# Closing the last chunk of a time-mixing layer in two halves, with the first expert's weights held behind its rows

## The reference

```python
# time mixing, per head
S = w_t * S + k_t v_t ;  y_t = r_t (S + u k_t v_t)
y = (y - mu) * rsqrt(var + eps) * ln_g + ln_b
x = layernorm(x + y @ W_o)                      # x1 below
# experts: capacity C = ceil(T * 2 / 32 * 1.2), T = 8192 tokens: 615 rows
top_w, top_i = top_k(softmax(x @ gate_w + gate_b), 2)
pos = how many earlier (token, choice) pairs took the same expert      # dropped if pos >= C
ye = gelu(xe @ w1 + b1) @ w2 + b2
x = layernorm(x + sum over the 2 choices of weight * ye)
```

## Time and profile before

| | |
|---|---|
| median of 3 runs | 2318.22 us (2316.73 to 2318.42) |
| the profiled execution | 2315.27 us, span 2313.5 us from first to last instruction |
| mean granted TensorE clock | 0.931 of full speed |
| busy share of the span | TensorE 83%, VectorE 78%, GpSimd 60%, ScalarE 47% |

### The profile page before, as it was taken

The page is one execution under the profiler, slowest core; times in us unless marked ns, Lnnn a source line. Parts: engine busy times, 40 slices in busy tenths (PEclk is TensorE's granted clock), DMA queues, the critical chain, the costliest instruction groups (busy, mean ns, idle before and its releaser), DMA issues. The chain is left out here.

```text
span 2313.5 us, 30790 instructions
## 1 busy us (share of the span) xinstructions
PE 1918.6 (83%) x9894; PEld 1327.6 (57%) x9894; DVE 1806.9 (78%) x3029; ACT 1097.8 (47%) x2143; POOL 1378.8 (60%) x954
## 2 busy tenths in 40 slices
PE   5887888787877878788865399999999999999980
PEld 2333343343433433333322299999999999999980
DVE  2899999999999999999995266666666666666655
ACT  2244554445444554445443255555555555555546
POOL 4667787777877887778874134444444444454440
PEclk9899999999999999999976599999999999999995
DMA  6832111121112111211110245554545545455537
GB/s 168 220 88 64 51 42 53 49 63 30 55 45 61 41 45 37 61 49 37 41 52 30 85 96 123 122 122 121 122 121 122 124 121 122 120 123 120 122 60 291
DMA packets 160569, 209.27 MB, mean 90 GB/s; under 512 B 12796, under 2 KB 136096, under 8 KB 160480
## 3 DMA queue, kind: packets, MB, share of 16 engines
q1 hardware_dynamic: 106544, 143.09, 21.1%
q0 software_dynamic: 28672, 34.78, 8.8%
q10 hardware_dynamic: 25264, 30.33, 4.9%
HBM read 118.65 MB, written 75.53 MB: 84 GB/s over the span
## 5 line engine op out<-in xcount | busy, mean ns | idle before, releaser
L801 DVE TENSOR_TENSOR_SCAN S<-wT,S,vb 128x512 f32<-128x512 f32 x512 | 624.9, 1262 | 0.0
L1075 POOL TENSOR_TENSOR prod<-S,rT 128x2048 f32<-128x2048 f32 x128 | 536.6, 4200 | 136.4 <-DVE S L801 135.8
L1294 PE MATMUL up<-x_parts,w_parts 128*128 128x308 f32 x3072 | 463.8, 307 | 1.5 <-DVE x_parts L1407 1.5
L1309 PE MATMUL down<-w_parts,h_parts 128*128 128x512 f32 (+1 forms) x1280 | 452.2, 396 | 0.0
L1294 PEld LDWEIGHTS up<-x_parts,w_parts 128*128 128x128 f32 x3072 | 438.9, 189 | 4.1 <-issue 1.8
L1369 POOL TENSOR_TENSOR ye<-ye,weight 128x256 f32<-128x256 f32 (+1 forms) x160 | 197.6, 1235 | 380.7 <-DVE ye L1463 380.7
L1347 ACT ACTIVATE h_full<-up,b_now 128x616 f32<-128x616 f32 x256 | 198.5, 776 | 420.8 <-PE up L1294 420.0
L1377 POOL DMA_INDIRECT sums<-ye,sum_at x160 | 283.8, 1773 | 146.5 <-POOL ye L1369 136.9
L1450 DVE TENSOR_TENSOR h_parts<-h_full,h_parts 128x616 fp32r<-128x616 f32 x256 | 206.7, 807 | 193.4 <-ACT h_parts L1347 193.2
L1312 PE MATMUL down<-w_parts,h_parts 128*128 128x256 f32 (+1 forms) x1280 | 357.3, 279 | 0.0
L794 DVE TENSOR_TENSOR vb<-vb,kT 128x512 f32<-128x512 f32 x512 | 327.9, 686 | 26.3 <-PE vb L575 26.2
(11 more groups left out here) (180 smaller groups left out, 2669.7 us busy)
## 6 DMA issues: line engine op xcount, KB each, us to landing
w_raw<-in_L_ffn_w_dram SPq DMA_DIRECT2D x64, 1024.0 KB, 8.8
expert_in_rows<-y_tok ACTq DMA_DIRECT2D x30, 652.5 KB, 9.2
xe<-expert_in_rows SPq DMA_DIRECT2D x32, 522.0 KB
v_stack<-v_parts SPq DMA_DIRECT2D x64, 256.0 KB, 4.5
x_tok<-in_L_attn_x_dram SPq DMA_DIRECT2D x16, 512.0 KB, 3.8
x_res<-in_L_attn_x_dram SPq DMA_DIRECT2D x16, 512.0 KB, 3.8
sums<-x_row SPq DMA_DIRECT2D x16, 512.0 KB, 2.9
rows<-sums SPq DMA_DIRECT2D x16, 512.0 KB, 6.8
```

Of the source, the lines that this page charges most:

```text
L801: dve.tensor_tensor_scan(line[:, 1:TC + 1], wT[:, par, half, :], vb[:, p % 2, g, :], line[:, 0:1], ALU.mult, ALU.add).then_inc(scanned, 1)
L1075: pool.tensor_tensor(prod[:, q % 2], S[:, q % RING, :, 0:TC], rT[:, par, half, None, :].to_broadcast([P, QUAD, TC]), ALU.mult).then_inc(pr ...
L1294: last = pe.matmul(up[:, f % 2, half, 0:HC], w1_parts[:, par, wp, k, f * P:(f + 1) * P], x_parts[:, par, xp, k, half * HC:(half + 1) * HC] ...
L1309: pe.matmul(down[0:m, (par * TILES + t) % 2, :, :], h_parts[:, 0, f, t * P:t * P + m], w2_parts[:, par, :, f, :], start=f == 0, stop=False)
```

## The change

The last chunk's closing steps no longer go through `stage_c`. Each engine has a `last_c` of its own, in which every step is done for two halves of two tiles, k = 0 and 1, each with a bank of `pa` (free by then; the gate uses banks of `vb`) and with 18 new semaphores. VectorE measures and normalizes both norms (statistics, inverse, one subtract-and-scale instruction for each tile), where ScalarE did most of that; ScalarE keeps roots, gain and bias, copies and weights. VectorE also works out the slot numbers. GpSimd is left with the copy of row numbers and the eight scatters, four behind each half. SP stores `x1` in two halves. The counters that only later chunks would need are left out. In `experts`, SP waits at expert 0 until both parts of its rows have landed before it issues `b2` and everything behind it.

```diff
@@ -409,11 +429,14 @@
-            store_x1(NCHUNK - 1)
-            sp.wait_ge(x1_stored, 16 * NCHUNK)
-
+            for k in range(2):
+                sp.wait_ge(half_normed, TPC + 2 * (k + 1))
+                sp.dma_start(sums[SPARE + (NCHUNK - 1) * TC + k * HALF:SPARE + (NCHUNK - 1) * TC + (k + 1) * HALF, :]
+                             .rearrange("(q p) c -> p q c", p=P), x1[:, 2 * k:2 * k + 2, :]).then_inc(x1_stored, 16)
+            sp.wait_ge(x1_stored, 16 * (NCHUNK + 1))
...
+        def chunks(eng, body, stage_a, tail):
...
             body(NCHUNK - 1, 1, False, True)
-            for s in range(SLOTS + 1):
-                stage_c(NCHUNK - 1, 1, s)
+            tail(NCHUNK - 1, 1)
...
@@ -611,11 +633,54 @@
 
-            def last_c(i, par, s):
-                if s == 0:
-                    for q in (NQ - 2, NQ - 1):
-                        reduce_y(i, par, q)
-                stage_c(i, par, s)
+            def last_c(i, par):
+                for q in (NQ - 2, NQ - 1):
+                    reduce_y(i, par, q)
+                pe.wait_ge(y_summed, stage_value(i, NH, NH))
+                for k in range(2):
+                    for t in range(2):
+                        for h in range(NH):
+                            last = pe.transpose(pa[:, k, t * C + h * P:t * C + (h + 1) * P],
+                                                y_sum[:, h, (2 * k + t) * P:(2 * k + t + 1) * P], ident[:])
+                    last.then_inc(half_turned, 1)
+                for k in range(2):
+                    pe.wait_ge(half_normed, 2 * (k + 1))
+                    for h in range(NH):
+                        for t in range(2):
+                            last = pe.transpose(pa[:, k, h * 2 * P + t * P:h * 2 * P + (t + 1) * P],
...
+                            last = pe.matmul(pa[:, k, t * C:(t + 1) * C], yT[:, h, at:at + P],
...
+                                                x1[:, 2 * k + t, h * P:(h + 1) * P], ident[:])
+                    last.then_inc(half_back, 1)
+                for k in range(2):
+                    pe.wait_ge(half_ready, 2 + k + 1)
+                    for t in range(2 * k, 2 * k + 2):
+                        for h in range(NH):
+                            last = pe.matmul(vb[:, 0, k, t * E:(t + 1) * E], yT[:, h, t * P:(t + 1) * P],
...
+                for k in range(2):
+                    pe.wait_ge(half_hits, k + 1)
...
+                        last = pe.matmul(pa[:, k, t * E:(t + 1) * E], before[:], hits[:, t, :], start=False, stop=True)
+                    last.then_inc(half_counted, 1)
@@ -807,7 +872,97 @@
-            chunks(dve, body, stage_a, stage_c)
+            def last_c(i, par):
+                def measure(src, k, which):
+                    for t in range(2 * k, 2 * k + 2):
+                        dve.bn_stats(stats[:, t, :], src(t)).then_inc(half_measured, 1)
+                    dve.wait_ge(half_measured, which * TPC + 2 * (k + 1))
+                    dve.sem_inc(wait_carrier, 1)
+                    for t in range(2 * k, 2 * k + 2):
+                        dve.bn_aggr(mv[:, t, :], stats[:, t, :]).then_inc(half_mean, 1)
+
+                def normalize(to, src, k, which):
+                    dve.wait_ge(half_rooted, which * 2 + k + 1)
+                    dve.reciprocal(rstd[:, which, 2 * k:2 * k + 2], rstd[:, which, 2 * k:2 * k + 2]
+                                   ).then_inc(half_inverted, 1)
+                    dve.wait_ge(half_inverted, which * 2 + k + 1)
+                    for t in range(2 * k, 2 * k + 2):
+                        dve.tensor_scalar(to(t), src(t), mv[:, t, 0:1], rstd[:, which, t:t + 1],
+                                          ALU.subtract, ALU.mult).then_inc(half_normed, 1)
+
+                def turned(t):
+                    return pa[:, t // 2, (t % 2) * C:(t % 2 + 1) * C]
+
+                for k in range(2):
+                    dve.wait_ge(half_turned, k + 1)
+                    measure(turned, k, 0)
+                for k in range(2):
+                    normalize(lambda t: y_tok[:, t, :], turned, k, 0)
+                dve.wait_ge(res_loaded, stage_value(i, 16, 16))
+                wait_from(dve, x1_stored, stage_value(i, 16, 0))
+                wait_from(dve, scattered, stage_value(i, 16 * 2 * TPC, 0))
+                for k in range(2):
+                    dve.wait_ge(half_mixed, k + 1)
+                    dve.tensor_tensor(x1[:, 2 * k:2 * k + 2, :], pa[:, k, :].rearrange("p (t c) -> p t c", t=2),
+                                      x_res[:, 2 * k:2 * k + 2, :], ALU.add).then_inc(half_added, 1)
+                    dve.wait_ge(half_added, k + 1)
+                    measure(lambda t: x1[:, t, :], k, 1)
+                for k in range(2):
+                    normalize(lambda t: x1[:, t, :], lambda t: x1[:, t, :], k, 1)
+                wait_from(dve, placed, stage_value(i, NPLACE, 0))
+                for k in range(2):
+                    dve.wait_ge(half_gated, k + 1)
+                    dve.tensor_tensor(logits[:, two], vb[:, 0, k, 2 * k * E:(2 * k + 2) * E]
+                                      .rearrange("p (t e) -> p t e", t=2),
+                                      gate_bias[:, None, :].to_broadcast([P, 2, E]), ALU.add).then_inc(half_chosen, 1)
...
+                    dve.tensor_tensor(hits[:, two], onehot[:, 0, two], onehot[:, 1, two], ALU.add
+                                      ).then_inc(half_hits, 1)
+                for k in range(2):
+                    two = slice(2 * k, 2 * k + 2)
+                    dve.wait_ge(half_counted, k + 1)
...
+                    at = 5 * k
+                    dve.tensor_scalar(slot_f[:, two], row_experts[:, two], float(CAP), None, ALU.mult
...
+                    dve.wait_ge(half_placed, at + 4)
+                    dve.tensor_copy(put_slot[:, two], slot_f[:, two]).then_inc(half_placed, 1)
+
+            chunks(dve, body, stage_a, last_c)
 
@@ -998,10 +1153,35 @@
+            def last_c(i, par):
+                def root(k, which):
+                    act.wait_ge(half_mean, which * TPC + 2 * (k + 1))
+                    act.activation(rstd[:, which, 2 * k:2 * k + 2], mv[:, 2 * k:2 * k + 2, 1], ACT.Sqrt,
+                                   bias=eps_col[:, 0:1]).then_inc(half_rooted, 1)
...
+                keep_y(i, 1)
+                for k in range(2):
+                    root(k, 0)
+                for k in range(2):
+                    act.wait_ge(half_back, k + 1)
+                    for h in range(NH):
+                        ins = act.activation(yT[:, h, k * HALF:(k + 1) * HALF], pa[:, k, h * HALF:(h + 1) * HALF],
...
+                for k in range(2):
+                    act.wait_ge(half_chosen, 8 * k + 6)
+                    act.activation(ratio[:, 2 * k:2 * k + 2], gap[:, 2 * k:2 * k + 2], ACT.Tanh, scale=0.5
...
@@ -1124,7 +1304,25 @@
-            chunks(pool, body, stage_a, stage_c)
+            def last_c(i, par):
+                wait_from(pool, scattered, stage_value(i, 16 * 2 * TPC, 0))
+                pool.wait_ge(row_moved, i)
+                pool.sem_inc(wait_carrier, 1)
+                pool.tensor_copy(x1_row[:, :, C + ROW_AT], sum_row[:]).then_inc(rows_set, 1)
+                for k in range(2):
+                    pool.wait_ge(half_weights, 2 * (k + 1))
+                    pool.wait_ge(half_placed, 5 * (k + 1))
+                    pool.wait_ge(rows_set, 1)
+                    pool.sem_inc(wait_carrier, 1)
+                    for t in range(2 * k, 2 * k + 2):
+                        for c in range(2):
+                            pool.indirect_dma_start(
+                                out=xe_dram[:, :],
+                                out_offset=bass.IndirectOffsetOnAxis(ap=put_slot[:, t, c:c + 1], axis=0),
+                                in_=x1_row[:, t, :], in_offset=None, bounds_check=NSLOT - 1, oob_is_err=False
+                            ).then_inc(scattered, 16)
+
@@ -1231,6 +1429,9 @@
                 sp.dma_start(xe[0:REST, par, FULL, :], xe_dram[bass.ds(at + FULL * P, REST), :]
                              ).then_inc(x_loaded[par], 16)
                 wait_from(sp, y_kept, stage_value(e, TILES, -TILES))
+                if isinstance(e, int) and e == 0:
+
+                    sp.wait_ge(x_loaded[0], 32)
                 sp.dma_start(b2_sb[:, par], b2[bass.ds(e, 1)].rearrange("e c -> (e c)").partition_broadcast(P)
                              ).then_inc(b2_loaded[par], 16)
```

More of the change, by code:

```diff
@@ L116, in time_mix @@
     SLOTS = 2 * NPAIR
+    HALF = TC // 2
     CAP = expert_slots(NTOK, E)
@@ L269, in time_mix @@
         weights_set = sem("weights_set")
+        half_turned = sem("half_turned")
+        half_measured = sem("half_measured")
+        half_mean = sem("half_mean")
+        half_rooted = sem("half_rooted")
+        half_inverted = sem("half_inverted")
+        half_normed = sem("half_normed")
+        half_back = sem("half_back")
+        half_ready = sem("half_ready")
+        half_mixed = sem("half_mixed")
```

(48 more changed lines are left out.)

53 lines of the change are left out of this document (added).

## The result

The changed kernel takes 2302.5 us (median of 4 runs, 2300.58 to 2306.42), the kernel before 2317.47 beside it (4 runs, 2315.86 to 2318.42): ratio 0.994, 95% interval 0.9928 to 0.9953. That is 11 to 17 us less, by the medians 15.0; 10.5 were forecast, 2307.7 with a range of 2301 to 2312. The profiled execution took 2306.42 (span 2304.7), the longest of the four runs.

What follows compares the result with a forecast made beforehand. The bound was taken as the last chunk's uncovered closing chain before a TensorE-bound expert part. Closing -14.0, experts' start +2.6 and clock +0.9 sum to -10.5 us: 2307.7 us, range 2301 to 2312 (own range 2304 to 2310.5).

Steps and rivals of the forecast that it cites:

- The bound: Last chunk's closing up to the experts' start: one chain, almost nothing covered, 57.4 us, adding one for one.
- The tail: Last chunk's first transposes to the experts' first load, 57.4 us before: 14.0 us less, ends 12.5 and 16.0.
- the landing: Chunk 14's last scatter, issued at 1264.99, lands up to 4.0 us later (least 2.4); taken as 1268.9.
- the spare time put in between the halves' scatters: Last chunk's eight scatters: an extra set of waits in the middle, up to 0.6 us, beside 9.05.
- The wait that binds: VectorE's first add in the last chunk waits for chunk 14's scatters reading x1_row; the chain loses some 2 us.
- The wait on SP: Expert 0's start: holding back w2 gains nothing for the rows and costs 2.6 us (from 1.5).
- The clock's share: Experts' start: TensorE's clock can stay longer at the lower level; 0.9 us added, between nothing and 2.
- One of the signs of being wrong: Wrong if rows land in 6 us, scatters move under 10, or clock rises after the third set of up products.
- The sum: Whole kernel: -14.0 + 2.6 + 0.9 = -10.5 us, 2307.7 when put on the median.
- the wait that helps: Rival at expert 0: w2 shared bandwidth, rows land some 3 us earlier, start gains 0 to 3; 2302.7; chance 0.14.
- the case without overlap: Rival in the last chunk's closing: halves don't overlap, last scatter 4 us later; 2311.7; chance 0.16.
- The clock: Rival at the experts' start: TensorE's clock stays low, deciding from 21 us extra; 2323 and more; chance 0.04.

Runs made afterwards that it cites:

- the first half placed first: Changed kernel with VectorE placing the first half straight after its choice, ahead of the second half's choice: 2303.36 us, ratio 0.9940.

## Why the prediction was right, step by step

**The bound.** That the tail is one chain and adds to the time holds, one for one to within some 3 us: with the overlap taken out, the tail gives back 10.8 us and the time 13.4 by the medians (2316.25 against 2302.9). Of the 2.6 beyond it, 1.5 lie in the third pair's start (27.20 against 25.71, the profiled executions), where the clock was down again. With the first half placed first, 1.6 less in the tail did not show in the time at all.

**The tail** was put at 14.0 less and came out 16.5 less, just beyond the upper end of 16.0, whose two conditions (an early landing of the scatter, the clock rising in the products) both came true. Counted from the first transposes: the add at 12.92 (14.1 forecast, from the slower of the two landings in rows 4, 4.0; the last scatter landed 2.4 behind its issue, and the first half's lead was lost as said); add to the first half of the gate 8.34 (8.65); from there to the first scatter 6.46 (6.95); the eight scatters 8.96 (9.5, since the second half's waits cost nothing: 1.28 between the fourth and fifth); the last scatter to the first load 4.20 (4.17). The mis-sized terms are the landing, 1.2 us, and the spare time put in between the halves' scatters, 0.5; the small steps on VectorE and GpSimd make up the rest.

**The wait that binds** is as forecast, and its price was put too low: about 2 us, measured 3.0 at the add and 0.8 more behind it by TensorE's clock. The forecast took the products at the lower clock throughout (two halves of 3.7). By the windows of the changed kernel the granted clock was 0.50 from 1260 up to 1266, 0.93 at 1266 to 1267 and 1.00 at 1267 to 1269; both halves together took 5.18, the second ended 1.5 us ahead of the add, and so VectorE waited for the scatters alone.

**The wait on SP.** That w2 delayed the rows by no more than 0.2 to 0.5 us, far less than the wait costs, is shown from three sides: taken out, put in alone, and with the rows spread, where the delay is gone. The third set came 3.2 later (2.6 forecast), since w2 landed at 15.64 where 15.2 was forecast and the chain from there to the gelu is 4.91. That 15.2 came so near is partly luck: w2 went out 0.6 earlier than forecast and took 6.8 to land, not 5.8. That expert 1's rows come later too, and hold TensorE ahead of the third set, was not in the prediction; it cost some 0.2 in the first profile, where the third set starts 1.67 behind the first gelu, and 1.49 to 1.50 where the gelu alone holds it. With the rows split they are there in time (turned at 14.39 with the wait), and the third set waits for the gelu alone. The clock's share, 0.9 with 0 to 2 as bounds, was 0 in one profile and 1.5 in another. One of the signs of being wrong, a clock that rises later than the third set, came half true: in the first profile the clock had risen to 1.00 at 1314, fell back to 0.50 in the third set and rose again only at 1324.

**The sum**, -10.5, was 4.5 us short of the medians' difference. The median of 2302.5 lies within the range of 2301 to 2312, which also took in the wait that helps and most of the case without overlap, but below the 2304 to 2310.5 that the forecast gave for itself; so that the range held is in part luck. The two profiled executions differ by 8.9 only, where 10.5 was forecast: 16.5 less in the tail, 4.7 more at the start, 0.9 more behind it, and 2.1 more ahead of the closing. The last does not look like the change's doing: the first transposes came at 1254.80 in the profile of before, at 1256.43 in the kernel before with the wait alone, and between 1255.87 and 1257.89 in all others; there is only one profile of the kernel before. Tail and start together give 11.8 less in the first profile of the changed kernel (16.5 and 4.7) and 13.5 in the second (16.4 and 2.8), both inside the interval of 11 to 17; the rest up to the medians' 15.0 was not followed up.

**The rivals.** By its number alone the wait that helps would have won: it stood at 2302.7, and 2302.5 was measured. It falls with the wait alone (1.0019) and with the split rows; the wait brings the rows forward by 0.2 to 0.5 us, not 3, and sets w2 back by 3.5 to 4.0 as long as the rows are not split. The halves do overlap, and that is the larger part of the gain. The clock did cost 1.5 us at the start in some executions, far from the 10.5 that it would have needed.

## What to carry to other kernels

Where the end of a stage is one chain through all engines, try splitting its steps in halves with a bank each: here that was worth more (10.8 us) than the rest of the change to the chain (5.7). Then look for the next bound among the waits that the old chain was late enough not to meet, here a buffer that older transfers still read. Before a load is held back to make way for another, look at the DMA share in the last microseconds of the one that is to gain: where that is the share of one engine, its own shape may be what sets its landing, and splitting it is the thing to try first. Here 96 and 7 partitions in place of 103 brought the rows forward by 4.1 us, the way made free by 0.2 to 0.5. And where a forecast and a rival give nearly the same time, only the order of events in the profile tells which is true.

## What the runs showed of the hardware

The transfer of 103 partitions kept the DMA share at 0.07 (22 to 24 GB/s) for some 4 us; the same rows as 96 and 7 brought the use of the rows from 8.51 to 4.37 us behind the first load. The Trainium skill ("DMA: Bandwidth & Descriptors", section on why a DMA increments its semaphore by 16) gives the rule by which 103 partitions go to one engine and 96 to sixteen; these runs agree with it: a share of 0.07 with the 103, 0.94 where the 96 landed.

In every profile chunk 14's second scatter starts 4.2 to 4.3 us behind the first, while in the profile of before the other chunks' are 1.37 to 1.54 apart. Of the changed kernel:

```profile
1255.27 1.07 POOL L1288 DMA_INDIRECT expert_in_rows<-x_row,put_slot  x1 [0.88 <-POOL put_slot L1279]
...
1259.50 0.99 POOL L1288 DMA_INDIRECT expert_in_rows<-x_row,put_slot  x1 [3.17 <-issue]
```

What holds GpSimd there was not tried and stays open. It lies ahead of the scatters for which the first add waits.
